# A transformer layer on one core: the first layer norm's statistics in two batches with set starts instead of three

## The reference

```python
q, k, v = split_heads(x @ Wq + bq), split_heads(x @ Wk + bk), split_heads(x @ Wv + bv)   # 16 heads of 16
q, k = favor(q), favor(k)         # p = exp(x - max(x)); p / (sum(p) + 1e-6), over each head's 16 features
probs = einsum('bhld,bhmd->bhlm', q, k) / (sum(q) + 1e-6)
x = layernorm(x + (einsum('bhlm,bhmd->bhld', probs, v) @ Wo + bo))      # the first layer norm
gate, up = fp4_linear(x, w_gate), fp4_linear(x, w_up)                   # 256 -> 704
x = layernorm(x + fp4_linear(silu(gate) * up, w_down))                  # 704 -> 256, the second one
```

## Time and profile before

| | us |
|---|---|
| median of 3 runs | 748.45 (747.55 to 748.8) |
| the profiled execution's own time | 746.88 |
| its span in the trace | 745.0 |
| PE busy | 705.5 |
| DVE busy | 621.3 |
| POOL busy | 558.7 |
| ACT busy | 552.5 |

### The profile page before, as it was taken

The page is one execution under the profiler, slowest core; times in us unless marked ns, Lnnn a source line. Parts: engine busy times, 40 slices in busy tenths (PEclk is TensorE's granted clock), DMA queues, the critical chain, the costliest instruction groups (busy, mean ns, idle before and its releaser), DMA issues.

```text
span 745.0 us, 16619 instructions
## 1 busy us (share of the span) xinstructions
PE 705.5 (95%) x4908; PEld 673.7 (90%) x4908; DVE 621.3 (83%) x1530; ACT 552.5 (74%) x1227; POOL 558.7 (75%) x585
## 2 busy tenths in 40 slices
PE   6999999999999978699999999999999999999984
PEld 5899999998888867699999999999999999999984
DVE  5988999899989976798788788787899887898784
ACT  5677777777899877467777777666666688788777
POOL 4677777776777686668878888788788788788761
PEclk9999999999999989899999999999999999999998
DMA  5222222222222110000000000000000011110114
GB/s 155 65 79 79 72 80 79 75 75 80 65 79 75 41 29 1 0 3 1 1 1 1 2 1 2 1 2 2 1 1 2 15 36 37 44 44 30 58 64 135
DMA packets 40045, 30.04 MB, mean 40 GB/s; under 512 B 3474, under 2 KB 39956, under 8 KB 39956
## 3 DMA queue, kind: packets, MB, share of 16 engines
q1 hardware_dynamic: 37508, 26.75, 12.0%
q10 hardware_dynamic: 2448, 2.23, 1.1%
HBM read 20.58 MB, written 8.39 MB: 39 GB/s over the span
## 4 chain that ended last, share of the span: by engine, by line
PE 81%; issue 6%; POOL 4%; DVE 4%; ACT 2%; DMA 1%; SPq 0%; ACTq 0%; POOLq 0%; DVEq 0%
PE bank L869 62%; PE wide L980 5%; PE wide L869 5%; PE bank L939 3%; PE bank L987 2%; PE bank L937 2%; PE wide L926 2%; POOL scratch L398 1%; POOL scratch L384 1%; PE bank L917 1%; DMA scratch<-L_attn_Wv 1%; POOL scratch L441 1%; ACT scratch L507 1%; DMA out<-scratch 1%; POOL scratch L407 0%
## 5 line engine op out<-in xcount | busy, mean ns | idle before, releaser
L869 PE MATMUL bank<-wf_hi,rounded 128*128 128x352 f32 (+1 forms) x1792 | 402.8, 310 | 12.7 <-DVE wf_lo L752 6.1
L869 PEld LDWEIGHTS bank<-wf_hi,rounded 128*128 128x128 f32 x1792 | 301.0, 190 | 15.4 <-DVE wf_lo L752 6.3
L869 PE MATMUL bank<-wf_lo,rounded 128*128 128x352 f32 (+1 forms) x896 | 274.2, 306 | 0.0
L869 PEld LDWEIGHTS bank<-wf_lo,rounded 128*128 128x128 f32 x896 | 170.7, 191 | 0.0
L441 POOL TENSOR_TENSOR scratch<-scratch 128x704 f32<-128x704 f32 x64 | 94.7, 1479 | 80.3 <-DVE scratch L825 76.6
L869 PE MATMUL bank<-qkv_hi,rounded 128*128 128x512 f32 (+1 forms) x512 | 147.5, 343 | 3.0 <-ACT bank L481 3.0
L869 PEld LDWEIGHTS bank<-qkv_hi,rounded 128*128 128x128 f32 x512 | 92.9, 190 | 13.7 <-issue 4.1
L426 POOL TENSOR_TENSOR scratch<-scratch 128x704 bf16<-128x704 f32 x64 | 99.4, 1553 | 7.7 <-ACT scratch L620 5.9
L390 POOL TENSOR_TENSOR rounded<-scratch,rounded 128x256 fp32r<-128x256 f32 x64 | 46.9, 734 | 60.8 <-ACT rounded L478 60.8
L794 DVE TENSOR_TENSOR scratch<-scratch,bank 128x352 f32<-128x352 f32 x64 | 33.2, 519 | 69.5 <-ACT scratch L581 67.2
L446 POOL TENSOR_TENSOR scratch<-scratch 128x704 f32<-128x704 bf16 x64 | 89.0, 1390 | 0.7 <-DVE scratch L829 0.7
(11 more groups left out here) (102 smaller groups left out, 1526.7 us busy)
## 6 DMA issues: line engine op xcount, KB each, us to landing
scratch<-x_feat SPq DMA_DIRECT2D x64, 128.0 KB, 2.2
scratch<-x_tok SPq DMA_DIRECT2D x64, 128.0 KB, 2.1
out<-scratch SPq DMA_DIRECT2D x64, 128.0 KB, 1.7
scratch<-w_ffn ACTq DMA_DIRECT2D x17, 128.0 KB, 2.2
scratch<-L_attn_Wq SPq DMA_DIRECT2D x1, 256.0 KB, 3.0
scratch<-L_attn_Wk SPq DMA_DIRECT2D x1, 256.0 KB, 3.2
scratch<-L_attn_Wv SPq DMA_DIRECT2D x1, 256.0 KB, 5.4
wo<-L_attn_Wo SPq DMA_DIRECT2D x1, 256.0 KB, 4.2
```

What stands on the lines that cost most here:

```text
L869: last = pe.matmul(dst, x(c), w(c), start=first and n == 0, stop=n == len(terms) - 1, skip_group_check=not first)
```

## The change

The first layer norm has two batches: tiles 0 to 23, whose 13 operations begin in step 32 with one per step (slot 4), and tiles 24 to 63, from step 72 with two per step. The start is now a column of the batch table, instead of the end of the batch plus a lag; the second norm's starts come out as before (38, 54, 62, 66, 70). The four statistics buffers have 40 columns instead of 32. `run` becomes one loop, with attention steps kept until group NS + 14 - 1, which issues nothing new but the later normalisations; all else keeps its order. By `ready` the steps are now:

- tiles 0 to 23: operations in steps 32 to 44, one per step; normalised in steps 45 to 78, two tiles in every three steps or fewer, never two in a step
- tiles 24 to 63: operations in steps 72 to 78, two per step (the last step one); normalised in steps 79 to 118, one per step

```diff
-LN_SLOTS = {2: (1, 5), 3: (0, 3, 6), 4: (0, 2, 4, 6), 7: (0, 1, 2, 3, 4, 5, 6)}
-LN_A = ((0, 32, 2), (32, 16, 2), (48, 16, 4))
-LN_B = ((0, 32, 2), (32, 16, 2), (48, 8, 4), (56, 4, 7), (60, 4, 7))
+LN_SLOTS = {1: (4,), 2: (1, 5), 3: (0, 3, 6), 4: (0, 2, 4, 6), 7: (0, 1, 2, 3, 4, 5, 6)}
+LN_A = ((0, 24, 1, 32), (24, 40, 2, 72))
+LN_B = ((0, 32, 2, 38), (32, 16, 2, 54), (48, 8, 4, 62), (56, 4, 7, 66), (60, 4, 7, 70))
...
-        ln_v = sb("ln_v", [P, 8 * T])
+        ln_v = sb("ln_v", [P, 10 * T])
...
-        A_FROM, A_LOOP, A_TO = -1, (4, NS - 1), NS + 7
-        B_FROM, B_LOOP, B_TO = -2, (6, NS - 2), NS + 3
+        A_FROM, A_LOOP, A_TO = -1, (4, NS - 1), NS + 14
+        B_FROM, B_TO = -2, NS + 3
         JOIN = NS + 1
-        A_LN, B_LN = 8, 6
...
-            starts = [first + count + lag + -(-LN_OPS // pace) for first, count, pace in batches]
+            starts = [start + -(-LN_OPS // pace) for _, _, pace, start in batches]
             spans = [later - start for start, later in zip(starts, starts[1:])] + [batches[-1][1]]
...
-                    at = slots.index(k) + pace * (m - first - count - lag)
+                    at = slots.index(k) + pace * (m - start)
...
-            for i in range(A_FROM, A_LOOP[0]):
-                attention(i)
-            for i in range(*A_LOOP):
-                attention(i)
-            for i in range(A_LOOP[1], A_TO):
+            for i in range(A_FROM, JOIN + B_TO):
                 for t in range(T):
-                    attention(i, [t])
+                    if i < A_TO:
+                        attention(i, [t])
                     if i - JOIN >= B_FROM:
                         ffn(i - JOIN, [t])
-            for i in range(A_TO - JOIN, B_LOOP[0]):
-                ffn(i)
-            for i in range(*B_LOOP):
-                ffn(i)
-            for i in range(B_LOOP[1], B_TO):
-                ffn(i)
```

More of the change, by code:

```diff
@@ L85, in layer_kernel @@
         nbias = sb("nbias", [P, NT])
-        ln_v = sb("ln_v", [P, 8 * T])
-        ln_h = sb("ln_h", [P, 8 * T], U32)
-        ln_t = sb("ln_t", [P, 8 * T])
-        ln_u = sb("ln_u", [P, 8 * T])
+        ln_v = sb("ln_v", [P, 10 * T])
+        ln_h = sb("ln_h", [P, 10 * T], U32)
+        ln_t = sb("ln_t", [P, 10 * T])
+        ln_u = sb("ln_u", [P, 10 * T])
         ident = sb("ident", [P, P])
@@ L220, in layer_kernel, with ready, ln_ops @@
         block = ctx.enter_context(nc.Block())
-        A_FROM, A_LOOP, A_TO = -1, (4, NS - 1), NS + 7
-        B_FROM, B_LOOP, B_TO = -2, (6, NS - 2), NS + 3
+        A_FROM, A_LOOP, A_TO = -1, (4, NS - 1), NS + 14
+        B_FROM, B_TO = -2, NS + 3
         JOIN = NS + 1
-        A_LN, B_LN = 8, 6
-        def ready(m, batches, lag):
-            starts = [first + count + lag + -(-LN_OPS // pace) for first, count, pace in batches]
+        def ready(m, batches):
+            starts = [start + -(-LN_OPS // pace) for _, _, pace, start in batches]
             spans = [later - start for start, later in zip(starts, starts[1:])] + [batches[-1][1]]
-            return [(g, first + k) for g, (first, count, _) in enumerate(batches) for k in range(count)
+            return [(g, first + k) for g, (first, count, _, _) in enumerate(batches) for k in range(count)
                     if starts[g] + k * spans[g] // count == m]
-        def ln_ops(k, m, batches, lag):
-            for g, (first, count, pace) in enumerate(batches):
+        def ln_ops(k, m, batches):
+            for g, (_, _, pace, start) in enumerate(batches):
                 slots = LN_SLOTS[pace]
                 if k in slots:
-                    at = slots.index(k) + pace * (m - first - count - lag)
+                    at = slots.index(k) + pace * (m - start)
                     if 0 <= at < LN_OPS:
@@ L561, in attention @@
                         squares(m - 8, 0, a_res, a_sq)
-                    for g, n in ready(m, LN_A, A_LN):
+                    for g, n in ready(m, LN_A):
                         normalise(n, res[:, rows(n)], a_ln, LN_OPS * (g + 1), a_x1)
@@ L588, in ffn @@
                         squares(m - 6, 1, y_s, y_sq)
-                    for g, n in ready(m, LN_B, B_LN):
+                    for g, n in ready(m, LN_B):
                         need(act, st_out[n % T], 16 * (n // T))
@@ L641, in layer_norm @@
             def layer_norm(k, g, batches, norm, done, sq):
-                n, count, _ = batches[g]
+                n, count = batches[g][0:2]
                 at = slice(n, n + count)
@@ L673, in ln @@
                     def ln(k):
-                        for at, g in ln_ops(k, m, LN_A, A_LN):
+                        for at, g in ln_ops(k, m, LN_A):
                             layer_norm(at, g, LN_A, 0, a_ln, a_sq)
@@ L780, in ln @@
                     def ln(k):
-                        for at, g in ln_ops(k, m, LN_B, B_LN):
+                        for at, g in ln_ops(k, m, LN_B):
                             layer_norm(at, g, LN_B, 1, y_ln, y_sq)
```

## The result

The changed kernel takes 744.02 us (median of 6 runs, 742.86 to 746.02); beside it the kernel before took 748.87 us (747.55 to 750.79). The ratio is 0.9933, 95% interval 0.9918 to 0.9949: 5.0 us less, between 3.8 and 6.1. I had forecast 744.3 us and 4.15 us less. Runs repeated later with the same two programs gave 0.9938 (0.9921 to 0.9954), and the kernel before against itself 1.0002 (0.9991 to 1.0013).

What follows compares the result with a forecast made beforehand. Attention was taken as a chain stretched by DVE and ACT, the feed-forward half as bound by PE. Gains 2.9 + 1.35 - 0.1 = 4.15 us, off 748.45, gave 744.3 us; range 742.5 to 746, 8 in 10 741.0 to 748.4.

Steps and rivals of the forecast that it cites:

- the mechanism in attention: Attention: a chain that DVE and ACT stretch whenever they get more work; first layer norm costs 5.7 us there.
- (b): Hand-over, step 72: two statistics operations instead of three ahead of wf_lo release PE 0.45 us earlier.
- (c): Hand-over, steps 74 to 78: two operations cost 0.9 us in each of steps 74 and 76; loses 0.2 us.
- New cost: Attention, tiles 32 to 44: 13 operations, one per step ahead of the reciprocal, cost 2.5 us; old cost 3.5.
- The normalisations: Attention, steps 45 to 63: 14 single normalisations on ACT cost 0.3 us instead of 2.2, gaining 1.9 us.
- (a): Hand-over, steps 67 and 71: one normalisation instead of two ahead of L604 and L581, 1.1 us gained.
- The feed-forward half: Feed-forward: added normalisations mostly hidden in ACT's idle time; 0.1 us lost beside the second norm's batch.
- C: Rival, attention: each of 13 operations waits for POOL and passes it on whole, 9.1 us; 750.9 us, chance 0.10.
- B: Rival, hand-over: even-step statistics stay on the chain, tiles 8 and 10 cost 2.6 us more; 746.9 us, chance 0.10.
- A: Rival: wf_lo stall no longer lowers PE's clock (1.6 us), or new operations fall in gaps (2.5); 742.7 or 741.8, chance 0.12.
- D: Rival: little gain, operations cost 3.5 us, normalisations 1.0, hand-over returns half; 746.7 to 748.4 us, chance 0.10.
- Its third part: Rival D's claim for the hand-over: held by POOL, it returns only half of the forecast gain.

Runs made afterwards that it cites:

- e2: Changed kernel with the first batch's 24 normalisations done two per step in steps 48 to 59: 746.02 us, ratio 0.9951.
- again: The changed kernel profiled once more, unedited: 744.64 us, ratio 0.9938.
- e1: Changed kernel with the first batch's 13 operations one place later, behind the reciprocal that releases POOL's scaling: 745.52 us, ratio 0.995.
- e5: Changed kernel with the last wf_lo (step 72) in front of the two statistics operations instead of behind them: 743.3 us, ratio 0.9923.
- e7: Changed kernel with three batches (24, 16, 24 tiles), 39 statistics operations, each normalisation kept in its step: 745.55 us, ratio 0.9954.
- e8: Changed kernel with e4's batches, the second with two operations in each odd step from 73, wf_lo in its old place: 739.98 us, ratio 0.9869.
- e3: Changed kernel with the second batch at four operations per step, steps 72 to 75: 745.1 us, ratio 0.9938.
- e4: Changed kernel with batches of 28 and 36 tiles, both at one operation per step, from steps 36 and 72: 740.13 us, ratio 0.9874.
- e6: Changed kernel with the batches of e4 and the wf_lo move of e5 together: 739.13 us, ratio 0.9864.

## Why the prediction came out

The total was right, 744.3 forecast and 744.02 measured, and so was the mechanism in attention and for parts (b) and (c) of the hand-over. But its sizes were off by 0.8 us in attention and by 1.1 the other way in the hand-over; that they cancelled is luck.

**Attention: 2.9 forecast, 3.74 measured.** The step "New cost" put 2.5 us on the 13 operations ahead of the reciprocal; tiles 32 to 45 take 1.44 us more than clean ones (0.95 to tile 40, 0.49 after). Nothing at t=0, as forecast; 0.28 at t=1 for 0.3; 0.20 at t=2 for 0.45; nothing at t=3 for 0.1. At t=1 the reading was right: the reciprocal starts 0.27 us later than it would. At t=2 two things were off. The reciprocal is held by 0.41 us, not 0.65, since the longer t=1 step lets POOL's L392 start 0.22 us before the operation and not with it; and DVE gets 0.21 back at L694, which takes 0.50 us for 0.71. The normalisations cost about 0.4 us for the forecast 0.3: 0.10 at each t=2 step from tile 46 to 58 (3.69 us for 3.59), not at t=1, where I had looked for it. (Tile 62 takes 3.75 us in every changed kernel, e2 too, which has no normalisation in that step.) That ACT was what stretched tiles 48 to 55 was shown by e2.

**The hand-over: 1.35 forecast, 0.2 measured** (108.48 us from tile 63 to F12, against 108.68, the mean of two profiles that lie 1.4 apart; by single waits and steps it is 0.6). Part (b), 0.45, is the wait's 6.10 to 5.66. Part (c), a loss of 0.2, is 1.57 against 0.81 + 0.98. What failed is part (a), 1.1 us for the normalisations in front of L604 and L581. At step 67 ACT was indeed earlier, and nothing came of it: from tile 63 to F0 it takes 20.98 and 20.93 us for 20.76 and 20.89. PE's transpose, ACT's copy and DVE's of the kernel before (L987, L604, L850), with what DVE did just before (L815):

```profile
273.58 0.38 PE L987 MATMUL bank<-ident,scratch 128*128 128x128 f32 x2
...
274.58 1.05 DVE L815 TENSOR_TENSOR scratch<-scratch 128x512 bf16<-128x512 f32 x1
...
275.22 0.36 ACT L604 ACTIVATE rounded<-bank 128x256 fp32r<-128x256 f32 x1
...
275.61 0.42 DVE L850 TENSOR_TENSOR rounded<-bank,rounded 128x256 fp32r<-128x256 f32 x1
```

and of the changed kernel:

```profile
269.58 0.38 PE L977 MATMUL bank<-ident,scratch 128*128 128x128 f32 x2
...
270.28 0.36 ACT L594 ACTIVATE rounded<-bank 128x256 fp32r<-128x256 f32 x1
...
270.92 0.69 DVE L805 TENSOR_TENSOR scratch<-scratch 128x512 bf16<-128x512 f32 x1
...
271.54 0.41 DVE L840 TENSOR_TENSOR rounded<-bank,rounded 128x256 fp32r<-128x256 f32 x1
```

ACT's copy starts 0.70 us behind the transpose instead of 1.64, DVE's 1.96 instead of 2.03. In the kernel before ACT's copy ended at 275.58 and DVE's L815 at 275.63, so DVE would have come no sooner without ACT's delay; in the changed kernel L805 still runs until 271.61. I had counted a delay on ACT as a delay of PE without asking when DVE would have come.

At step 71 part (a) holds, smaller. F2 to F3 takes 7.62 and 7.63 us with two normalisations in that step (the kernel before), 7.25 to 7.28 with one (changed, again, e1, e5, e7, e8) and 6.68 or 6.69 with none (e2, e3, e4, e6). The change went from two to one and gained 0.37 for the forecast 0.54; the second one would be worth 0.57. The forecast, then, had 0.7 us too much in part (a): 0.54 at step 67, and 0.17 at step 71. The other 0.4 down to the measured 0.2 lies within the spread.

**The feed-forward half: 0.1 us of loss forecast, 0.05 measured** (F12 to F63, 349.99 against 349.93). F45 to F51, with three normalisations a step, takes 41.09 us against 41.08.

**The rivals.** C, that each of the 13 operations waits and passes it on whole, had its threshold at 0.51 us an operation; measured are 0.11 on average. The wait for POOL is real and as long as the operation's place says: DVE's operation of 142.36 + 0.49 us ends 0.03 us behind POOL's L392 (142.14 + 0.68), and that of e1, 140.85 + 0.98, 0.03 behind POOL's scaling. The Trainium skill ("SBUF — State Buffer", Who interferes with whom) says that of two instructions of DVE and POOL that both need their shared port the later is blocked for the whole of the earlier; these two ends agree. But the wait was mostly for short rests, and most of it did not reach the end. B, the even steps, charged tile 8 with 2.5 us and tile 10 with 1.0; PE waited 0.98 and nothing. A's clock part: with the wait at 5.66 us the clock fell as before (0.66 granted in the 7 us behind it). Even after 3.56 to 3.65 us (e5, e6, e8) it fell, to 0.76, though e5's and e8's first matmul still ran at full speed. "TensorE: Matmul & The Clock Gate" (What's actually happening) in the Trainium skill ties the clock to how busy the engine has lately been; the traces agree in that it fell behind each of these waits, but how much is lost differs between two executions of one program. D is out for attention: neither the operations nor the normalisations cost what it said. Its third part, that the hand-over returns half, was nearer than my own sum, though not for its reason (POOL).

## What to carry to other kernels

Where small dependent operations must run beside a busy pipeline, choose their place in each engine's step by what the other engines do at that moment, one at a time; the same 13 operations cost 2.3 us in pairs, 1.4 us singly in the right slot, and at the hand-over two in an even step made PE wait 0.8 to 1.0 us where two in an odd step, or one in either behind wf_lo, cost nothing. Before booking a gain from an engine that becomes free earlier, look at the next engine's own queue: if it would come at the same time anyway, nothing is gained. And look for what stands behind the moved work on its engine: here a piece of weights that PE waited 6 us for. When comparing two profiles, measure between marks inside the program and read the granted clock beside each stretch. The version with both batches at one per step and that piece moved forward takes 739.1 us, 1.4% less than the kernel before.

## What the runs showed that I had not expected

One program, profiled twice, with the same wait of 6.1 us on PE, spent 3.4 us of the next 7 at 1.2 GHz in one execution and 6.2 in the other, and was 1.3 us longer for it from F3 to F12. The time up to tile 24 varies by 2.7 us between executions of programs that are the same there (101.3 to 104.1 us). And an operation that waits a full microsecond for POOL (e1, t=1) costs the step only 0.9, while its neighbour at t=2, waiting for nothing, makes its step 0.2 us shorter than a clean one with nothing added (3.37 against 3.59). The rows say how: in the clean t=2 step POOL's scaling starts 2.45 us behind the row maximum (158.76 against 156.31), because POOL is still in L402; in e1, behind a longer t=1 step, POOL is done with that instruction sooner and the scaling starts 2.24 us in (144.66 against 142.42), so DVE's L694 meets less of it (0.42 us for 0.71).
